# The fill of the edge pass: a power of its own for the first three chunks, and the preset of the row table at the fourth chunk's transposes

## What is computed

```
def _layernorm(x, axis=-1, eps=1e-05): return (x - mean) / jnp.sqrt(var + eps)
ft = jnp.einsum('nhd,od->nho', hv, W)
a1 = jnp.sum(ft * attn_l, axis=-1)
a2 = jnp.sum(ft * attn_r, axis=-1)
e = jax.nn.leaky_relu(a1[src] + a2[dst], negative_slope=NEG_SLOPE)
w = jnp.exp(e - m[dst])
alpha = w / jnp.maximum(denom[dst], 1e-16)
agg = jax.ops.segment_sum(alpha[:, :, None] * ft[src], dst, num_segments=n)
out = jax.nn.relu((agg + res).reshape(n, H * DOUT))
...
x = x + _L0_gnn_ref(_layernorm(x, axis=-1), src, dst, ...)
x = x + _L0_ffn_ref(_layernorm(x, axis=-1)[None], ...)[0]
```

## Time and profile before

| | |
|---|---|
| median of 3 runs | 2722.25 us (2721.98 to 2723.72) |
| the profiled execution's own time | 2722.58 us |
| its span, first to last instruction | 2720.8 us |
| mean granted clock of TensorE | 0.989 |
| busy: PE, DVE, ACT, POOL | 97%, 88%, 87%, 78% |
| PE in the first of 40 slices of the span | 5 tenths |

### The profile page before, as it was taken

One profiled execution on the slowest core, in us unless ns is written; L12 is line 12 of the kernel. 1 busy time (PEld: TensorE's weight loads), 2 busy tenths in 40 slices (PEclk: granted clock), 3 DMA queues, 4 the chain that ended last, 5 costly groups with the idle time before them and its releaser, 6 DMA issues. The chain is left out here.

```text
span 2720.8 us, 69258 instructions
## 1 busy us (share of the span) xinstructions
PE 2628.0 (97%) x21450; PEld 2389.0 (88%) x21450; DVE 2397.0 (88%) x4890; ACT 2378.5 (87%) x4748; POOL 2135.0 (78%) x2029
## 2 busy tenths in 40 slices
PE   5999999999999985999999999999999999999998
PEld 4888888888888864899999999999999999999997
DVE  4688888888888876999999999999999999999996
ACT  4988888888888863999999999999999999999993
POOL 7777777777777615888888888888888888888882
PEclk9999999999999997999999999999999999999999
DMA  8677777787777646899999999999999999989883
GB/s 314 215 259 254 254 252 253 252 252 253 254 253 255 217 149 245 313 350 341 333 332 330 324 321 324 324 317 315 317 321 314 314 319 315 311 312 312 315 311 119
DMA packets 254177, 777.86 MB, mean 286 GB/s; under 512 B 77185, under 2 KB 85165, under 8 KB 253837
## 3 DMA queue, kind: packets, MB, share of 16 engines
q1 hardware_dynamic: 184190, 563.88, 58.4%
q0 software_dynamic: 69312, 210.37, 25.0%
q10 hardware_dynamic: 432, 0.62, 0.1%
HBM read 638.86 MB, written 236.65 MB: 322 GB/s over the span
## 5 line engine op out<-in xcount | busy, mean ns | idle before, releaser
L1017 PE MATMUL ps<-wr_bd,arena 128*128 128x128 f32 x4704 | 592.7, 276 | 19.1 <-DVE arena L1390 19.0
L1017 PEld LDWEIGHTS ps<-wr_bd,arena 128*128 128x128 f32 x4704 | 563.0, 193 | 20.5 <-issue 20.4
L702 POOL DMA_INDIRECT arena<-agg_scratch,nrow x392 | 438.9, 1120 | 76.7 <-issue 67.5
L644 POOL TENSOR_SCALAR arena<-csr_neg,mv,r_n 128x768 f32<-128x768 f32 x392 | 388.2, 990 | 50.9 <-PE ps L859 37.9
L1385 DVE SCALAR_TENSOR_TENSOR ps<-ps,r_n,arena 128x768 f32<-128x768 f32 x392 | 398.9, 1018 | 16.6 <-DMA arena<-agg_scratch,nrow 15.5
L809 ACT ACTIVATE t_hi<-ps 128x768 fp32r<-128x768 f32 x392 | 314.3, 802 | 95.4 <-PE ps L859 95.2
L818 ACT ACTIVATE arena<-arena,s_st 128x768 f32<-128x768 f32 x392 | 363.6, 928 | 30.5 <-DVE arena L1390 30.5
L1390 DVE SCALAR_TENSOR_TENSOR arena<-ps,arena 128x768 f32<-128x768 f32 x392 | 375.3, 957 | 13.4
L692 POOL TENSOR_SCALAR arena<-arena,nm_n,r_n 128x768 f32<-128x768 f32 x392 | 382.6, 976 | 2.7 <-issue 1.9
L1397 DVE TENSOR_TENSOR t_lo<-ps,t_hi 128x768 fp32r<-128x768 f32 x392 | 373.7, 953 | 10.2 <-ACT t_hi L809 10.2
L777 ACT ACTIVATE arena<-arena,mv 128x768 f32<-128x768 f32 x392 | 367.4, 937 | 12.8
(11 more groups left out here) (213 smaller groups left out, 6218.9 us busy)
## 6 DMA issues: line engine op xcount, KB each, us to landing
arena<-in_x SPq DMA_DIRECT2D x196, 768.0 KB
arena<-in_x_cols SPq DMA_DIRECT2D x392, 384.0 KB, 5.0
out<-arena SPq DMA_DIRECT2D x195, 768.0 KB, 5.7
agg_scratch<-agg_ring SPq DMA_DIRECT2D x196, 384.0 KB, 3.8
dst_all<-in_dst_rows SPq DMA_DIRECT2D x28, 256.0 KB, 3.7
arena<-agg_scratch,nrow POOLq DMA_INDIRECT x392
arena<-in_x,e_slot POOLq DMA_INDIRECT x364, 4.6
dst_all<-in_dst_rows SPq DMA_DIRECT2D x28, 192.0 KB
```

What stands on the lines that cost most here:

```text
L644: pool.tensor_scalar(g_ring[:, g, :].rearrange("p (c f) -> p c f", f=P), csr_neg[:, None, :].to_broadcast([P, NC, P]), mv1[:, w, 2 * (v % ...
L702: pool.indirect_dma_start(g_ring[:, g, :], None, agg_d, bass.IndirectOffsetOnAxis(nrow[:, v, 3:4], 0), bounds_check=EP - 1, oob_is_err=Fal ...
L1017: last = nc.tensor.matmul(res_ps(b, tr)[:, i * P:(i + 1) * P], xt_ring[:, g, i * P:(i + 1) * P], wr_bd[:], start=True, stop=True)
```

## The change

- The first three chunks (E0 = 3) get a ve_s, a power and a nm_s of their own; the other four chunks of the first group share another set. s_ve, s_rp and s_nm count one more from there on.
- DVE takes the statistics of chunks 0 and 1 before it copies PE's first result (L1103), those of chunk 2 behind that copy, then the new ve_s; the new nm_s stands behind csr_neg.
- POOL's order in the fill: from step 3 on one source and one target gather each, with the target three chunks behind. The power for three chunks stands in step 4, that for four at the end of step 7, that of the second group at the end of step 15 rather than 18.
- The preset is issued inside SP's loop, at step 13, once four chunks are transposed (s_tr at 12). POOL waits for it at step 17, ahead of the first scatter.
- w1_sb and w2_sb lie in agg_ring, slots 0 and 1.

```
+E0 = 3
...
+        w2_sb = agg_ring[0:HID + 1, 0, :]
+        w1_sb = agg_ring[:, 1, 0:NC * HID].rearrange("p (c h) -> p c h", h=HID)
...
-            sp.wait_ge(s_rowinit, 1)
...
             for b in turns(sp, NB, 2):
                 for i in range(BODY):
+                    if isinstance(b, int) and b == 0 and i == BODY - 1:
+                        sp.wait_ge(s_rowinit, 1)
+                        sp.wait_ge(s_tr, 4 * NBLK)
+                        for a in range(BODY):
+                            sp.dma_start(row_parts[a], row_init).then_inc(d_rowinit, 16)
...
-                    if first and G <= c < G + 4:
-                        for v in (2 * (c - G), 2 * (c - G) + 1):
-                            gather_targets(v, v // G, e_all[:, v, 1:2])
-                    if exists(cd, EC) and not (isinstance(cd, int) and cd < 8):
+                    if first and c == E0 + 1:
+                        pool.wait_ge(s_ve, 1)
+                        pool.tensor_tensor(r_s[:, 0, 0:E0], ve_s[:, 0, 0:E0], half[:, 0:E0], ALU.pow).then_inc(s_rp, 1)
+                    if exists(cd, EC):
...
-                        if isinstance(b, int) and c == BODY:
+                        if isinstance(b, int) and c == BODY + DST_LAG:
                             pool.wait_ge(d_rowinit, 16 * BODY)
...
-                    if isinstance(b, int) and c == G + 1:
-                        pool.wait_ge(s_ve, 1)
-                        pool.tensor_tensor(r_s[:, 0, :], ve_s[:, 0, :], half[:, 0:G], ALU.pow).then_inc(s_rp, 1)
+                    if isinstance(b, int) and c == G:
+                        pool.wait_ge(s_ve, 2)
+                        pool.tensor_tensor(r_s[:, 0, E0:G], ve_s[:, 0, E0:G], half[:, E0:G], ALU.pow).then_inc(s_rp, 1)
+                    if isinstance(b, int) and c == BODY + 1:
+                        pool.wait_ge(s_ve, 3)
+                        pool.tensor_tensor(r_s[:, 1, :], ve_s[:, 1, :], half[:, 0:G], ALU.pow).then_inc(s_rp, 1)
...
-                        act.wait_ge(s_nm, 2 * b + (i - L_NORM) // G + 1)
+                        act.wait_ge(s_nm, 1 if isinstance(cn, int) and cn < E0 else 2 * b + (i - L_NORM) // G + 2)
...
+            for c in range(2):
+                source_stats(c, c, 0, c, 0)
             dve.wait_ge(l_const, 16 * NCONST)
...
-            for c in range(2):
-                source_stats(c, c, 0, c, 0)
+            source_stats(2, 2, 0, 2, 0)
+            dve.wait_ge(s_ag, E0)
+            V.tensor_scalar(ve_s[:, 0, 0:E0], mvs[:, 0, 0:E0, 1], EPS, None, ALU.add).then_inc(s_ve, 1)
...
+            dve.wait_ge(s_rp, 1)
+            V.scalar_tensor_tensor(nm_s[:, 0, 0:E0], mvs[:, 0, 0:E0, 0], -1.0, r_s[:, 0, 0:E0],
+                                   ALU.mult, ALU.mult).then_inc(s_nm, 1)
```

More of the change, by code:

```diff
@@ L189, in gnn_ffn_kernel @@
         coef = part(34252, 4, EC, rows=HEADS)
-        w2_sb = part(21504, D, rows=HID + 1)
-        w1_sb = part(24000, NC, HID)
         v_sb = part(24600, NC * (2 * HEADS + 2))
@@ L481, in _ @@
             sp.dma_start(row_i, dst_ends.rearrange("(o n) e -> o n e", o=1).to_broadcast([P, 2, EC])).then_inc(l_fix, 16)
-            sp.wait_ge(s_rowinit, 1)
             row_parts = row_d.rearrange("(a p n) o -> a p (n o)", a=BODY, p=P)
-            for a in range(BODY):
-                sp.dma_start(row_parts[a], row_init).then_inc(d_rowinit, 16)
             for b in turns(sp, NB, 2):
                 for i in range(BODY):
+                    if isinstance(b, int) and b == 0 and i == BODY - 1:
[3 more added lines that the diff above has]
+                            sp.dma_start(row_parts[a], row_init).then_inc(d_rowinit, 16)
                     for h, (at, lo, hi) in enumerate(((19, 0, 4), (22, 4, G))):
@@ L612, in _ @@
                         gather_targets(v, n, e_all[:, v, 1:2] if isinstance(cd, int) and cd < BODY else e_slot[:, e, kd, 1:2])
-                        at_least(pool, s_sum, c - BODY - L_SUM + L_TR + 1)
-                        settle(pool)
-                        if isinstance(b, int) and c == BODY:
+                        if not isinstance(cd, int) or cd >= 8:
+                            at_least(pool, s_sum, c - BODY - L_SUM + L_TR + 1)
+                            settle(pool)
+                        if isinstance(b, int) and c == BODY + DST_LAG:
                             pool.wait_ge(d_rowinit, 16 * BODY)
@@ L624, in _ @@
                             .then_inc(d_scat_first, 16)
-                    if isinstance(b, int) and c == G + 1:
-                        pool.wait_ge(s_ve, 1)
-                        pool.tensor_tensor(r_s[:, 0, :], ve_s[:, 0, :], half[:, 0:G], ALU.pow).then_inc(s_rp, 1)
+                    if isinstance(b, int) and c == G:
[4 more added lines that the diff above has]
+                        pool.tensor_tensor(r_s[:, 1, :], ve_s[:, 1, :], half[:, 0:G], ALU.pow).then_inc(s_rp, 1)
                     gp = 2 * b + (i - 11) // G
-                    if k == 11 % G and exists(gp, NG) and not (isinstance(gp, int) and gp == 0):
+                    if k == 11 % G and exists(gp, NG) and not (isinstance(gp, int) and gp < 2):
                         w = (i - 11) // G % 2
-                        pool.wait_ge(s_ve, gp + 1)
+                        pool.wait_ge(s_ve, gp + 2)
                         settle(pool)
@@ L1149, in _ @@
                         dve.wait_ge(s_ag, G * (gv + 1))
-                        V.tensor_scalar(ve_s[:, w, :], mvs[:, w, :, 1], EPS, None, ALU.add).then_inc(s_ve, 1)
+                        lo = E0 if isinstance(gv, int) and gv == 0 else 0
+                        V.tensor_scalar(ve_s[:, w, lo:], mvs[:, w, lo:, 1], EPS, None, ALU.add).then_inc(s_ve, 1)
                         if isinstance(gv, int) and gv == 0:
@@ L1159, in _ @@
                         w = (i - 8) // G % 2
-                        dve.wait_ge(s_rp, gn + 1)
+                        lo = E0 if isinstance(gn, int) and gn == 0 else 0
+                        dve.wait_ge(s_rp, gn + 2)
                         at_least(dve, s_norm, G * (gn - 1))
-                        V.scalar_tensor_tensor(nm_s[:, w, :], mvs[:, w, :, 0], -1.0, r_s[:, w, :],
+                        V.scalar_tensor_tensor(nm_s[:, w, lo:], mvs[:, w, lo:, 0], -1.0, r_s[:, w, lo:],
                                                ALU.mult, ALU.mult).then_inc(s_nm, 1)
@@ L1248, in _ @@
                             variances(q)
-                    if exists(c, EC) and not (isinstance(c, int) and c < 2):
+                    if exists(c, EC) and not (isinstance(c, int) and c < E0):
                         source_stats(c, i, i // G, k, 2 * b + i // G)
```

## The result

The changed kernel took 2736.91 us (median of five runs, 2736.01 to 2737.76); the kernel before, timed beside it, 2722.87. The ratio is 1.0046, 95% interval 1.0035 to 1.0057: 14.0 us slower, where +6.7 us was forecast and 2734 was the upper end of the range. The direction was right, the size was not. The profiled execution's span is 2735.1 us (own time 2736.91).

What follows compares the result with a forecast made beforehand. POOL's gathers were taken to pace the fill, PE everything after; the scatter, 11.1 us late behind POOL's waits and the preset, left 6.6 us after slack, plus 0.1 for the clock: +6.7, 2722.25 to 2729.0, range 2722 to 2734.

Steps and rivals of the forecast that it cites:

- what paces the fill: First 100 us: POOL, not PE, sets the pace, one gather per 1.25 us, with only 1.8 us idle to give back.
- from the scatter to r_d: First row scatter to the target side's first power: 22.6 us before, less 1.4 and 0.85; r_d 8.8 us later.
- from r_d to the end: After r_d, 8.8 us late: 6.0 us late on PE, 6.6 by the third group's power; the later counts.
- how long the preset takes: SP's 3.21 MB preset beside gathers: data from near 40, landing at 62, so POOL waits 5.5 us before the first scatter.
- estimate of 7.4 us: Preset's moving time worked out at 436 GB/s: there by 48, making the 5.5 us term zero; the forecast did not use it.
- the preset's start: SP, after the fourth chunk's norm (32.4) and transposes: preset starts at 38 to 39 us, its data near 40.
- the clock behind the new idle time: PE's slower transposes after idling, beside the wait for the third group's power: adds 0 to 1.5 us, taken as 0.1.
- 2.2 us of slack: Third group's power ended at 88.16, DVE used it at 90.33; this slack cuts its 8.8 us lateness to 6.6.
- its two paths: PE late through r_d and the scores (6.0 us) or through the third group's power (6.6 us); the latter was taken.
- POOL's waits: POOL before the first, second and third powers of the fill: new waits of 3.1, 1.3 and 0 us.
- the preset is in time: Rival: preset landed by 56, scatter at 56.4, +1.0 us, 2723.3, no change; chance 0.33 (in time or nearly).
- the waits are longer: Rival: fourth chunk lands at 7.3 us, first wait 4.0 us, everything moves 3 to 4 us: 2733; chance 0.12.

## Why the prediction was right and wrong

**Right: what paces the fill.** "The changed order keeps all DMAs ahead of both points, so a head start of PE meets POOL again there." The first norm came at 20.38 (forecast near 20), seven us earlier, and nothing was left of it. DVE then waited 15.43 us for r_d. In this kernel the preset lies on the way as well; what shows POOL's part by itself are the runs in the kernel before, where the second group's power moved alone gained nothing and all powers together 5.7 us.

**Right: from the scatter to r_d; right in number only: from r_d to the end.** After the late scatter r_d came 20.3 us behind (forecast 22.6 - 2.25 = 20.35). The forecast carried a scatter at 62 to +6.7 us, and with scatters at 61.57 and 62.13 the two kernels with an earlier preset lost 6.0 and 5.8. But the last part of the way was another than the forecast took, as shown below under the clock, so that this agreement is in part luck.

**Right in sum: how long the preset takes.** It was forecast from 40 to 62, 22 us (23 to 24 from its issue), with 0.105 MB per us beside gathers; it took 22.1 us from its issue at 46.49 to 68.60. The parts were off and cancelled, which is luck: until POOL was ready q1 moved 2.37 MB in 13.0 us, 0.18 MB per us (forecast 2.2 MB in 16.4 us), with gathers pausing for longer than was counted (from 57 to 59.5 us POOL's queue moved only 0.02 MB); then the rest took 9.09 us and not 5.5. (The prediction's 1.74 MB for 16.4 us at 0.105 should be 1.72; nothing hangs on it.) The estimate of 7.4 us, worked out from the figure in the Trainium skill's page "DMA: Bandwidth & Descriptors", section "Anatomy of one DMA", which describes a DMA that POOL issues, does not hold for SP's preset beside gathers here. The same page of the Trainium skill, section "Queues, rings and completion order", says that each DMA engine takes a packet from one queue and then one from the next. The trace agrees, here between 62 and 64 us of the kernel after:

```profile
q0 software_dynamic: 130, 0.61, 73.4%
q1 hardware_dynamic: 145, 0.23, 30.1%
```

With nearly equal counts, the preset's packets of 1.6 KB get 0.23 MB where the gathers' of 4.7 KB get 0.61, the ratio of the earlier trace rows again.

**Wrong: the preset's start.** The step that failed is "From the norm of a chunk to the end of its transposes it was ... 5.4 without the 1.3 us that the clock cost ... so the preset starts at 38 to 39". The norm was where it was forecast (32.96, forecast 32.4), but to the end of the transposes it took 13.4 us (to 46.4). The 6.7 us were read off chunk 7, where PE waits for ACT alone. At the fourth chunk PE first waits for DVE's copy of an earlier result, and DVE for the gathers of chunks 8 to 10, which the new order issues 6 to 12 us later. The prediction had named that copy, "in DVE's order, the copy that PE needs for each chunk", but for r_d alone. So the preset started some 8 us later than forecast (46.49), and as it took a little less from its issue than forecast, the scatter came 6.6 us later (68.60 instead of 62), which is 6.6 of the 7.3 us by which the sum was off.

**Wrong: the clock behind the new idle time.** It was put at 0 to 1.5 us and taken as 0.1. The granted clock between 91 and 96 us was 0.50 of 2.4 GHz, that is the 1.2 GHz level, after 12.21 us in which PE ran nothing; before, it was at the upper level, 2.4 GHz, there (first row after, second before, columns as in the earlier trace rows):

```profile
91.00:96.00 5.00, 4.15 (x26) 3.31 (x27) 3.90 (x15) 2.55 (x6) 3.78 (x5) 0.50 0.55 157
...
91.00:96.00 5.00, 3.84 (x42) 3.48 (x41) 3.77 (x9) 5.00 (x10) 4.09 (x4) 1.00 0.60 193
```

The scores were 12.6 us late, nm_s of the third group 14.7, the end 14.0: 0.8 us more than the forecast's chain, with its 2.2 us of slack, gives (15.4 us late at the third group's power, less 2.2, is 13.2). The forecast also took the wrong one of its two paths. It said that the third group's power counts, but in DVE's order nm_s stands behind work of the first group that follows from the scores, and there DVE waits 2.40 us for ACT; the row above at 103.86 shows it, and so does this one of the kernel before:

```profile
89.17 0.25 DVE L1275 TENSOR_SCALAR arena<-ps 128x84 f32<-128x84 f32 x1 [2.40 <-ACT arena L745]
```

So nm_s goes by the scores: 12.6 us late, and 2.1 us more because from the scores on PE to nm_s it took 13.63 us (91.38 to 105.01) instead of 11.53 (78.80 to 90.33), with PE at the lower clock in between (transposes 2.80 and products 1.96 us, at the upper level 1.51 each). That gives the 14.7. The clock's term was thus 2.1 us in that execution, outside its range of 0 to 1.5, and the 2.2 us of slack were no part of the path.

**Too small, but hidden: POOL's waits.** Forecast were waits of 3.1, 1.3 and 0 us, measured 4.03, 1.65 and 2.30, and the two short powers together took 2.17 us where 1.75 + 0.5 was put. POOL was ready for the scatter at 59.5 instead of 56.4. In the changed kernel this hid behind the preset's landing. It is what the rival "the preset is in time" was priced by: +1.0 us, where the kernels in which the preset is in time lost 6. So the chances of 0.33 for this rival and 0.35 for no change rested on a price that was too low, by 5 us as those kernels show and by 3 us (59.5 less 56.4) by the changed kernel's own waits.

**The range.** Its upper end, 11.75 us above before, came from "the waits are longer", which moves everything by 3 to 4 us. It looked for the delay on POOL and not on PE, where the preset's trigger sits, and there it was 6.6 us.

What stays open: which share of the remaining 6 us belongs to each of POOL's three waits or to the new order of gathers, which was never run without the split, and whether the power of three chunks gains anything once the later powers have moved.

## What to carry to other kernels

When a transfer is moved behind a semaphore, price its start on the engine that raises the semaphore: walk that engine's order back through every wait ahead of it, and those engines' orders too; here one chunk more in the condition lay behind a stall and cost 15.5 us of start and 8 us of the end. Price its length from rows of the same stretch, beside the same other traffic. And a wait that is taken away gains only what the next wait in line leaves: look for that one first, and move both (here +0.6 and +0.6 us alone, -5.7 together).

## What the runs showed of the chip

- A wait of PE of only 3.42 us was followed by the 1.2 GHz level, as one of 12.21 us was. In the kernel with the second group's power early the granted clock was 1.00 from 72 to 77 us, in which most of the wait lies, and 0.50 behind it, columns as in the earlier trace rows:

```profile
72.00:77.00 5.00, 2.03 (x19) 1.83 (x17) 0.46 (x3) 2.88 (x5) 4.19 (x5) 1.00 0.63 197
...
79.00:84.00 5.00, 5.00 (x24) 5.00 (x25) 3.93 (x15) 3.47 (x7) 3.80 (x4) 0.50 0.72 218
```

  Each of the two groups of 12 matmuls at that level took 1.3 us longer (2.80 and 2.81 instead of 1.51): 2.6 us of PE's time behind one short wait. Not all of it reached the end: nm_s of the third group came 1.15 us later than before (91.48 against 90.33).
- A power on POOL took 0.88 us for 128x3, 1.29 for 128x4 and 1.51 to 1.75 for 128x7, so that two short ones took 2.17 us where one full one takes 1.51 to 1.75.
- A gather's landing depends on what else runs, and not only on the preset: the median of the first 28 was 7.3 us in the kernel before and 5.1 with nothing but the preset moved out of their way. In the changed kernel's order it was 4.6, and still 4.9 with the preset back at its old place. Single ones show more than these medians: chunk 6's source took 4.7 us in the changed kernel and 7.3 with the preset at its old place, and chunk 1's, issued at 7.85 beside the constants in the changed kernel, 6.4 (statistics at 14.29).
